# A graph network kernel: fewer node products in layer 1, the rest in the output stage, and other queues for its transfers

## The reference

```python
h = maximum(layernorm(x), 0)
# relational layer: sum over edges of (h @ W[type]) into the target, plus a bias
x = x + segment_sum(einsum('ni,rio->rno', h, W)[type, src], dst) + h_bias
h = maximum(layernorm(x), 0)
h = leaky(h @ enc_w + enc_b)                       # leaky: v if v >= 0 else 0.1 v
for l in range(2):
    agg = segment_sum(h[src], dst) * inv_deg
    h = leaky(agg @ lin_l_w[l] + lin_l_b[l] + h @ lin_r_w[l])
x = x + h
```

## Time and profile before

| what | us |
|---|---|
| median of 3 executions | 3426.85 (3426.82 to 3428.76) |
| the profiled execution: own time | 3434.24 |
| its span | 3432.4 |
| relational stage | about 78 to 1109 |
| node stage | 1122 to 2171 |
| layer 1 | 2181 to 2814 |
| output stage | 2814 to 3432 |

### The profile page before, as it was taken

How to read it: one execution, slowest core, us unless ns; L and a number is a source line. 1 busy time by engine, 2 the same in 40 slices (tenths; PEclk the granted TensorE clock), 3 DMA queues, 4 the chain that set the end, 5 groups by cost and what they waited for, 6 DMA issues and landing times. The chain is left out here.

```text
span 3432.4 us, 57476 instructions
## 1 busy us (share of the span) xinstructions
PE 2372.6 (69%) x13942; PEld 1758.7 (51%) x13942; DVE 2910.6 (85%) x8326; ACT 1909.4 (56%) x4979; POOL 2497.7 (73%) x2364
## 2 busy tenths in 40 slices
PE   2999999999998688888888888488888860000000
PEld 2555555555554466666666666388778760000000
DVE  4999999899897799999999999699999966555665
ACT  1666666566665688888888888255555540000000
POOL 4777777777776677777777776677777747677675
PEclk9999999999999899999999999799999985555555
DMA  9988888886222899999999997599999979999998
GB/s 242 387 294 263 260 256 257 252 244 178 84 76 66 295 287 282 285 283 282 288 280 289 281 288 219 179 393 401 397 395 395 398 281 412 414 414 414 408 412 313
DMA packets 663813, 1016.37 MB, mean 296 GB/s; under 512 B 73669, under 2 KB 406343, under 8 KB 657058
## 3 DMA queue, kind: packets, MB, share of 16 engines
q1 hardware_dynamic: 487190, 555.28, 49.8%
q10 hardware_dynamic: 94758, 285.20, 21.5%
q0 software_dynamic: 81536, 172.20, 15.1%
HBM read 534.94 MB, written 485.83 MB: 297 GB/s over the span
## 5 line engine op out<-in xcount | busy, mean ns | idle before, releaser
L973 PE MATMUL y_ps_rel<-w_basis,ht_rel 128*128 128x512 f32 x1568 | 745.0, 598 | 0.1
L1722 POOL DMA_INDIRECT gat_l<-base_and_means,src_c x392 | 469.7, 1198 | 123.9 <-issue 118.8
L704 POOL DMA_INDIRECT agg<-rows_rel,put_c x392 | 410.8, 1048 | 135.5 <-issue 98.7
L1270 ACT ACTIVATE h_node<-base_node,shift_node,rstd_node 128x128 f32<-128x128 f32 x1176 | 500.5, 483 | 1.6 <-DVE shift_node L1360 1.6
L368 POOL DMA_INDIRECT gat_rel<-in_x_dram,src_c x392 | 403.7, 1030 | 125.0 <-issue 106.5
L1111 POOL DMA_INDIRECT base_and_means<-rows_node,odd_c x392 | 388.9, 992 | 145.3 <-issue 118.0
L1102 POOL DMA_INDIRECT term_node<-agg,src_c x392 | 395.1, 1008 | 132.9 <-issue 119.7
L1727 POOL DMA_INDIRECT means<-late_l,put_c x336 | 366.9, 1092 | 160.7 <-issue 94.2
L826 DVE SCALAR_TENSOR_TENSOR two_rel<-y_ps_rel,coef,two_rel 128x128 f32<-128x128 f32 x1568 | 437.5, 341 | 3.2 <-DVE two_rel L826 1.8
L973 PEld LDWEIGHTS y_ps_rel<-w_basis,ht_rel 128*128 128x128 f32 x1568 | 269.6, 192 | 192.0 <-issue 131.1
L1655 DVE TENSOR_TENSOR last_z_l<-last_z_l,node_done_l 128x1024 f32<-128x1024 f32 x98 | 120.2, 1226 | 255.9 <-DMA node_done_l<-means 255.8
(11 more groups left out here) (183 smaller groups left out, 5988.8 us busy)
## 6 DMA issues: line engine op xcount, KB each, us to landing
pairs_l<-base_and_means SPq DMA_DIRECT2D x196, 512.0 KB
base_and_means<-zero_row SPq DMA_DIRECT2D x49, 1024.0 KB
means<-zero_row SPq DMA_DIRECT2D x49, 1024.0 KB
first_node<-in_x_dram SPq DMA_DIRECT2D x196, 256.0 KB
term_node<-agg SPq DMA_DIRECT2D x196, 256.0 KB
x<-base_node SPq DMA_DIRECT2D x196, 256.0 KB
base_and_means<-done_node SPq DMA_DIRECT2D x196, 256.0 KB
z<-node_done_l ACTq DMA_DIRECT2D x196, 256.0 KB
```

Source lines behind the costliest of these rows:

```text
L704: nc.gpsimd.indirect_dma_start(agg, bass.IndirectOffsetOnAxis(ap=put_c[:, t:t + 1], axis=0), rows[:, q, j, :], None).then_inc(s_scattered[ ...
L973: nc.tensor.matmul(y_ps[(q + j) % 2][:, c * 512:(c + 1) * 512], ht[:, q, j, :], w_basis[:, 4 * c:4 * c + 4, :], start=True, stop=True).the ...
L1270: last = nc.scalar.activation(h[:, n % 2, j * P:(j + 1) * P], base[:, n % SLOTS, j * P:(j + 1) * P], ACT.Relu, bias=shift[:, b % 2, c:c + ...
L1722: nc.gpsimd.indirect_dma_start(gat[:, g, j, :], None, source, bass.IndirectOffsetOnAxis(ap=src_c[:, t:t + 1], axis=0)).then_inc(s_gathered ...
```

## The change

It does the following; line numbers with "new" are those of the changed file.

- *Relational stage.* `SPARE` is doubled. Its rows are zeroed in `agg` and in both halves of `pair` by two transfers that SP issues after the third half-step's spill (1.8 MB and 3.7 MB in rows of 512 bytes); before, 0.9 MB were zeroed at the end of SP's list. GpSimd's first scatter waits for both. The ring `rows` has three half-steps, and ACT waits for its slots once in a half-step. The seven aggregates and one addition of `mean_var` are five small operations.
- Waits of DVE, ACT and PE that other waits imply are gone, in all stages.
- *Layer 1.* The sweep does 4 blocks in two half-steps, 112 of the 196. Of these the first 98 are stored, the last 14 stay in `last_z` as parts 0 to 6.
- *Output stage.* Parts 7 to 48 (`AGAIN` = 42) have no z: their pair rows (1 MB each) are loaded, DVE adds and leaks them (`mix`, new L1660, L1663), PE turns and multiplies, DVE adds the means to the product in PSUM (new L1671). `mix` of the next part stands before `combine` of this one. All loads and stores are issued by SP. The means that return (new L1804) are issued by GpSimd two half-steps ahead, into four buffers. Part of the loads (x1 of parts 0 to 6, three parts of pair rows, the first four returning means) are issued amid or before the end of layer 1.

```diff
@@ relational stage
+                            if m == 0 and j == 0:
+                                pool.wait_ge(s_spare, 2 * DMA)
                             pool.wait_ge(s_rows, tile(m, j))
...
                             spill(m)
+                            if m == 2:
+                                sp.dma_start(agg[N:N + SPARE, :].rearrange("(p j) f -> p j f", p=P),
+                                             zero_row[:].unsqueeze(1).to_broadcast([P, SPARE // P, P])).then_inc(s_spare, DMA)
+                                sp.dma_start(pair[N:N + SPARE, :].rearrange("(p j) (k f) -> p (j k) f", p=P, f=P),
+                                             zero_row[:].unsqueeze(1).to_broadcast([P, SPARE // P * 2, P])).then_inc(s_spare, DMA)
...
-                            if at_least(m, 2):
-                                act.wait_ge(s_scattered[q][j], use(m - 2, q))
-                            nc.scalar.activation(rows[:, q, j, :], row_ps[:, 0:P], ACT.Copy).then_inc(s_rows, 1)
+                            if m >= KEPT and j == 0:
+                                act.wait_ge(s_scattered[m % KEPT], HALF * DMA * (m // KEPT))
+                            nc.scalar.activation(rows[:, m % KEPT, j, :], row_ps[:, 0:P], ACT.Copy).then_inc(s_rows, 1)
@@ layer 1
-                    return [[(0, 0), (2, 1), (4, 2), (6, 3)], [(1, 4), (3, 5), (5, 6)]][r]
+                    return [[(0, 0), (4, 1)], [(1, 2), (4, 3)]][r]
+                def stays(w, i, c):
+
+                    return i * w.walk + c >= STORED
@@ output stage
+                    for k in range(COUNT):
+                        if again(k + 1):
+                            mix(k + 1)
+                        combine(k)
...
+                    for k in range(SWEEP, SLOTS_OUT):
                         load(k)
+                    load_pair(SLOTS_OUT)
+                    sp.wait_ge(s_node_mixed, SWEPT)
+                    for k in range(SWEEP):
+                        load(k)
+                    sp.wait_ge(sweep.s_turn, SWEPT)
+                    wait_base(sp)
+                    sp.wait_ge(s_need, 1)
+                    sp.wait_ge(s_mixed, HALVES)
+                    for k in range(1, len(last_pair)):
+                        load_pair(SLOTS_OUT + k)
+                    sp.wait_ge(s_carried, T)
                     for k in range(COUNT + STORED_AFTER):
                         if k < COUNT:
                             load_means(k)
                         if k >= STORED_AFTER:
                             store(k - STORED_AFTER)
-                        if k + LOADED_BEFORE < COUNT:
+                        if again(k + LOADED_BEFORE) and k + LOADED_BEFORE >= SLOTS_OUT + len(last_pair):
+                            load_pair(k + LOADED_BEFORE)
+                        if SLOTS_OUT <= k + LOADED_BEFORE < COUNT:
                             load(k + LOADED_BEFORE)
...
+                            if m >= KEPT + 2:
+                                back(m + 2)
                             if m < KEPT:
                                 pool.wait_ge(s_rows, tile(edges, HALF - 1))
                             else:
-                                pool.wait_ge(s_back[q], use(m - KEPT, q))
+                                pool.wait_ge(s_back[slot], (turn_ + 1) * DMA)
```

More of the change, by code:

```diff
@@ L1501, in layer_pass @@
                     s_spilled = [psem(f"spilled{q}") for q in range(2)]
-                    s_back = [psem(f"back{q}") for q in range(2)]
-                    pairs = buf("pairs", [P, WALK, NB, 2 * P])
+                    s_back = [psem(f"back{q}") for q in range(4)]
+                    pairs = buf("pairs", [P, SWEEP, NB, 2 * P])
                     KEPT = 8
@@ L1670, in wait_base, with turn_again @@
[L1670 to L1676 removed]
+                    for k in range(COUNT):
+                        if again(k + 1):
+                            mix(k + 1)
+                        combine(k)
+                def turn_again(pe, n):
+                    pe.wait_ge(s_releaked, n + 1)
+                    for j in range(2 * NB):
+                        last = nc.tensor.transpose(ht_ps[j // NB][:, j % NB * P:(j % NB + 1) * P],
+                                                   last_z[:, n % WALK, j * P:(j + 1) * P], ident[:])
+                    last.then_inc(s_returned, 1)
@@ new lines, in keep_turned_again, with wait_final, wait_base @@
+                def keep_turned_again(act, n):
+                    act.wait_ge(s_returned, n + 1)
+                    for a in range(2):
+                        last = nc.scalar.activation(ht[:, a, :], ht_ps[a][:], ACT.Copy)
+                    last.then_inc(s_reht, 1)
+                def wait_final(sp, k):
+                    sp.wait_ge(s_final, sp.value_load(need[0:1, COUNT - 1 - k:COUNT - k], min_val=1, max_val=HALVES))
+                def wait_base(sp):
+                    for c in range(SWEEP):
+                        sp.wait_ge(sweep.s_stored[c], DMA * len(range(c, STORED, SWEEP)))
@@ L1696, in store @@
-                        act.dma_start(part(out, k), last_z[:, c, :]).then_inc(s_out[c], DMA)
-                    wait_base(act)
-                    for k in range(LOADED_BEFORE):
+                            sp.wait_ge(s_out[0], DMA)
+                        sp.dma_start(part(out, k), last_z[:, c, :]).then_inc(s_out[c], DMA)
+                    for k in range(SWEEP, SLOTS_OUT):
                         load(k)
+                    load_pair(SLOTS_OUT)
+                    sp.wait_ge(s_node_mixed, SWEPT)
@@ L1764, in _ @@
                         if l:
+                            for q in range(2):
+                                pool.wait_ge(s_spilled[q], DMA * ((HALVES - KEPT) // 2))
+                            for m in range(len(late_rows)):
+                                back(KEPT + m)
                             for m in range(HALVES):
@@ L1911, in _ @@
                             ago(HALVES, 0, 0, j, 4, finish)
-                        if l:
-                            write_out(act)
-                        else:
-                            for c in range(sweep.walk):
-                                act.wait_ge(sweep.s_stored[c], DMA * walks)
+                        for n in range(AGAIN):
+                            keep_turned_again(act, n)
                     @block.tensor
@@ L1956, in _ @@
                             ago(HALVES, 0, 0, j, 3, to_rows)
+                        for n in range(AGAIN):
+                            turn_again(pe, n)
+                            product_again(pe, n)
             clear(held)
```

317 lines of the change are left out of this document (158 added, 159 removed).

## The result

| | before | after |
|---|---|---|
| median, us | 3427.81 | 3394.69 |
| ratio, 95% interval | | 0.990 (0.988 to 0.992) |
| profiled execution: own time, span | 3434.24, 3432.4 | 3396.55, 3394.8 |
| first scatter | 103.4 | 127.9 |
| node stage's first gather | 1122.0 | 1147.3 |

The profiled spans differ by 37.6 us: +25.3 in the relational stage, -1.3 in the node stage, -80.4 in layer 1's gathers, -14.5 in the turn, +33.3 in the output stage. The forecast had +25, 0, -52, -20 and +18. So the sum came out by terms of which two were off by 28 and 15 us, in opposite directions. The profiled spans fell by 8.6 us more than the forecast's 29; the medians are nearer to it (33.1) because the two profiled executions stand 6.4 and 1.9 us above their medians. On both counts it is luck that the total came within 3 us.

A forecast was written before the change was run, and what follows sets the result against it. GpSimd was taken to bound the relational stage, DVE the node stage and layer 1, DMA the output stage. Terms +25 - 52 - 20 + 18 = -29 took the median 3426.85 to 3398 us; 8-in-10 range 3350 to 3450.

The forecast's parts named there:

- Relational stage: First stage: GpSimd's first scatter waits for the new zeroes until near 131.5 us; +25 us, bounds +15 to +28.
- the 4 us that I gave back: Relational stage: of GpSimd's 28 us wait, 1 us was there anyway and some 3 return at the stage's end.
- Layer 1: 84 blocks fewer on DVE, GpSimd next to be late: gathers at 9.5 us a half-step, -52 us, bounds -94 to +0.
- if the leak begins L after the half-step's last gather ... with L = 2 us: Layer 1: the next half-step's last gather ends at L + 8.1 or L + 6.9 in turn, mean 9.5 us.
- The rule for a single gather: Layer 1: a gather begun within DVE's two-input addition is held, ending 0.82 us after it; others take 0.94 us.
- gathers aren't held: Layer 1 rival: leaks fall between gathers or hold them less, 8.75 us a half-step; 3356 us, chance 0.17.
- Slower: collisions persist: Layer 1 rival: DVE's other two-input operations still hold gathers, mean stays 10.5 us a half-step; 3450 us, chance 0.17.
- The turn: From layer 1's last gather to the first put: shorter leak lag, one block fewer, last blocks not stored; -20 us, within 5.
- Output stage: From first put to end: bound by DMA, 254 MB at 413 GB/s plus idle start and end; +18 us, bounds +5 to +45.
- The rival of slow returns: Output stage: each returning load costs GpSimd 3 us instead of 1.3; +29 in all, 3456 us, chance 0.07.
- The chain through PE: Output stage: parts computed again pass DVE, PE and ACT in 7.7 us each at half clock, a tie with DMA.
- The node stage: Stage after the relational one: only waits that others imply are removed; 0 us, within 3.

The follow-up runs named there:

- e4: Changed kernel with 3 instead of 4 blocks in two half-steps of layer 1, 56 parts computed again: 3449.6 us, ratio 1.007 to the kernel before.
- e2: Changed kernel with all 196 blocks in layer 1 again (7 in two half-steps), no part computed again: 3435.0 us, ratio 1.004 to the kernel before.

## Why the forecast held, step by step

**Relational stage: the mechanism right, the size in part by luck.** GpSimd stood at the first scatter until the zeroes had landed, and nothing gave the time back. Of the working two figures were off. SP's transfers after, with the time to landing:

```profile
base_and_means<-zero_row SPq DMA_DIRECT2D x1, 3584.0 KB, 21.8
```

Issued at 105.8, it landed at 127.6, not 131.5. The window after (columns as in the earlier trace rows):

```profile
106.00:127.60 21.60, 20.85 (x88) 12.29 (x87) 20.43 (x85) 14.16 (x46) 0.00 (x0) 1.00 1.04 309
```

At 309 GB/s in all the engines moved 6.7 MB: the 5.5 MB of zeroes and little over 1 MB besides. I had put 2.4 MB ahead of them and zeroes at 270 GB/s behind. And of the 4 us that I gave back (1 at the wait, 3 at the end) none came back: the first scatter is 24.5 us later, the node stage 25.3. The two errors cancel.

**Layer 1: the step that failed is "if the leak begins L after the half-step's last gather ... with L = 2 us".** It took DVE to be waiting for gathers as soon as it had less work than GpSimd's free pace. I had 8.6 us for DVE's operations and 8.75 us for GpSimd, 0.15 apart, and left out DVE's own waits for PE in front of a carry (0.6 in every second half-step). With them DVE takes 8.96 in the stretch above, is the slower one still, and lags 7 to 11 us behind; the gathers fall into step with it and go at nearly its pace, 8.99. The rule for a single gather (held until 0.82 us after the end of an operation with two inputs in SBUF, if it starts within it) was right in these traces, with 0.92 in place of 0.82 behind the selection; where gathers start was wrong. The rival "gathers aren't held" was near in size (-94 for the -80 measured), while its reason (leaks between gathers) was half of it. e4 shows what my assumption would have cost where it is true. The rival "Slower: collisions persist" didn't come with four blocks; with three the whole came to its 3450, but with half-steps of 9.85, below the 10.1 from which it counts, and with an output stage that is longer by 15.6.

**The turn: -14.5 for -20, by the same step.** DVE after, the last leak and the last carry, to hold beside the earlier trace rows:

```profile
2728.63 1.08 DVE L1895 TENSOR_TENSOR act_gat_l<-gat_l 128x896 f32<-128x896 f32 x1
...
2737.18 0.80 DVE L1908 SCALAR_TENSOR_TENSOR sums_l<-open_l,sums_l,sum_ps_l 128x128 f32<-128x128 f32 x2 [0.62 <-PE sum_ps_l L1990]
```

From the last gather (2717.7) 11.0 us to the leak, for which I had 2 to 3, then 9.4 to the end of the last carry (10.4 forecast), and 5.6 in ACT (5 to 6 forecast without the stores). The 8 us are DVE's lag. The forecast's terms add to 17.4 to 19.4 us, not to 19 to 20: with its own sum the turn would have been off by more.

**Output stage: DMA bound as forecast, but +33 for +18.** The core moved 256.9 MB from the first put on, not 254: two of the three early pair parts were issued five us before it and moved within the stage:

```profile
2738.39 0.79 SPq L1742 DMA_DIRECT2D gat_l<-base_and_means  x2
```

At 413 GB/s that is 622 us. The idle start cost 13 as forecast (263 GB/s over 36 us, above), the end about 10: after the last put the rate is 349. The chain at the end has one transfer left, the means of the third part from the end, and then DVE's work:

```profile
3370.48 8.87 DMA act_gat_l<-means
```

I had 3 to 7 for the end and nothing for the middle, where the rate is 408, not 413: 7 us more. So the step that failed here is the sum's size: 6 us of bytes, 3 to 7 at the end, 7 in the middle. Before, too, the mean rate over the stage was 396 GB/s (244.7 MB in 618 us); the 12.2 MB that were in fact added are 31 us at that rate. With the 9.7 MB that the forecast had it would have given 24, nearer to 33 than 18.

**What doesn't bind there.** GpSimd ended its puts 68 us before the end, so the returns' price didn't matter. It was smaller than any bound that I set: the line of their issue after (duration in ns, least, median, most),

```profile
L1804 POOL DMA_DIRECT2D late_l<-means_by_edge x24: 589/597/618, 2717.7 to 3277.6; - x24
L1804 POOL DMA_DIRECT2D rows_l<-means_by_edge x24: 592/596/609, 2718.8 to 3299.3; - x24
```

gives 0.6 us for each of 48; I had taken 1.3. Of the 44 in the output stage 28 began within a DVE operation with two inputs in SBUF, of 1.2 us, some of them 0.1 us into it, and took no longer than the others. The rival of slow returns is refuted. The rule of the Trainium skill that plain transfers belong to ACT or SP (page "SBUF — State Buffer", section "SBUF: two separate sides") didn't bite: no issue was held. The Trainium skill ties the lock there to DVE operations in a 2-port mode, a condition that I had left out; whether any of these ran in it no row shows.

The chain through PE isn't late either. DVE's longest waits of the output stage after are for transfers, and PE's products aren't among them (total, times, longest):

```profile
DVE last_z_l L1676 <- DMA node_done_l<-means: 58.7, 28, 3.6
DVE last_z_l L1671 <- DMA node_done_l<-means: 33.4, 20, 2.9
```

The clock that I took for it was too low: with work on PE again, the granted clock was 0.64 over 2800 to 3380, not 0.50 (windows above).

**Loads and stores on SP.** e2 has the node blocks of the kernel before in both stages, with the new issue order: its output stage is 604.7 us, 13 below the 618.0 of before. It moves 237.3 MB in that stage instead of 244.7, as some loads come earlier and some parts stay in the chip; at 413 GB/s the 7.4 MB are 18 us. So the fewer bytes are enough for the gain, and none of it is shown to come from the queues or the four buffers.

**The node stage** went from 1059.0 to 1057.7 us: waits that others imply cost nothing there.

## What to carry to other kernels

Before an engine is relieved, compare its whole period, waits for third engines included, with the pace of the one that would be next; where the two are close they can run in step or trip over each other, and work taken away can then cost: three blocks were 55 us worse than four, where the sum of work had them 1 to 4 us worse. A wait in front of the first transfer of a stage that goes at one engine's pace cost its full length here (24.5 us, and 25.3 at the end of the stage); zeroing earlier took back 17 to 19 us at once. For a stage that the DMA engines bound, price added bytes at the stage's mean rate, start and end included, not at its peak.

## What the hardware showed that I had not expected

Less work on DVE can slow GpSimd: with three blocks instead of four, DVE was busy for 434 of 552 us and a gather took 1123 ns instead of 1004. A gather that starts within an operation with two inputs in SBUF ends 0.82 us after it (0.92 after the selection, one of whose inputs is uint8); one that starts up to 0.4 us ahead of it passes in 0.95. A plain load issued by GpSimd took it 0.59 to 0.62 us beside such operations, and none of 48 was held.
